# Graph attention kernel, first layer: a step's context is scaled on VectorE and added to the strip's sum on GpSimd

## The reference

```python
h = jnp.maximum(_layernorm(x, axis=-1), 0.0)
q, k, v = h @ Wq.T + bq, h @ Wk.T + bk, h @ Wv.T + bv      # split into 4 heads
kc = k.reshape(B, H, Nc, CHUNK, Dh)                          # 8 chunks of 256 keys
scores = jnp.clip(einsum('bhnd,bhjcd->bhnjc', q, kc) / sqrt(Dh), -10.0, 10.0)
scores = jnp.where(mask == 0, -10.0, scores)
attn = jax.nn.softmax(scores, axis=-1)                       # over each chunk by itself
ctx = jnp.einsum('bhnjc,bhjcd->bhnd', attn, vc)              # summed over the chunks
out = ctx @ Wo.T + bo + h                                    # then a layer norm, gamma, beta
x = x + out
```

## Time and profile before

| | |
|---|---|
| median of 3 runs | 4495.8 us (4494.7 to 4496.92) |
| the profiled execution's own time | 4492.85 us |
| its span, first to last instruction | 4491.0 us |
| PE busy | 4246.6 us (95%) |
| DVE busy | 4024.7 us (90%) |
| ACT busy | 2977.8 us (66%) |
| POOL busy | 714.7 us (16%) |
| granted TensorE clock, mean | 0.992 |

### The profile page before, as it was taken

The page is one execution under the profiler, slowest core; times in us unless marked ns, Lnnn a source line. Parts: engine busy times, 40 slices in busy tenths (PEclk is TensorE's granted clock), DMA queues, the critical chain, the costliest instruction groups (busy, mean ns, idle before and its releaser), DMA issues. The chain is left out here.

```text
span 4491.0 us, 168889 instructions
## 1 busy us (share of the span) xinstructions
PE 4246.6 (95%) x72733; PEld 3492.7 (78%) x72733; DVE 4024.7 (90%) x9728; ACT 2977.8 (66%) x3317; POOL 714.7 (16%) x613
## 2 busy tenths in 40 slices
PE   7999999999999999999999999969999999999998
PEld 5777777677677777777767777758999999999998
DVE  5998899889898899889988989978999999999998
ACT  5555555555555555555555555538999999999997
POOL 3121122112121122112211211110000010000100
PEclk9999999999999999999999999989999999999999
DMA  5100110011001010011011101113212122122221
GB/s 122 58 23 19 34 30 21 26 30 30 26 21 30 21 35 23 24 31 30 21 27 29 30 21 27 36 35 102 76 39 83 41 70 81 31 80 54 58 71 36
DMA packets 174046, 188.95 MB, mean 42 GB/s; under 512 B 7520, under 2 KB 157408, under 8 KB 173152
## 3 DMA queue, kind: packets, MB, share of 16 engines
q1 hardware_dynamic: 166192, 159.49, 12.8%
q0 software_dynamic: 7088, 18.36, 1.7%
HBM read 110.43 MB, written 38.03 MB: 33 GB/s over the span
## 5 line engine op out<-in xcount | busy, mean ns | idle before, releaser
L789 ACT ACTIVATE slot<-slot,shift 128x1024 f32<-128x1024 f32 x1024 | 1113.5, 1088 | 1184.5 <-PE slot L639 1176.2
L651 PEld LDWEIGHTS outs<-v_s,probs 128*64 128x64 f32 x32768 | 1042.2, 137 | 450.5 <-issue 271.3
L925 DVE SCALAR_TENSOR_TENSOR probs<-slot,bound 128x1024 f32<-128x1024 f32 x1024 | 1245.6, 1217 | 90.1 <-ACT slot L789 84.7
L651 PE MATMUL outs<-v_s,probs 128*64 128x66 f32 x32768 | 1179.5, 225 | 62.7 <-DVE ctx_sum L945 58.1
L1559 ACT ACTIVATE u<-s_all,d_sign 128x1024 bf16<-128x1024 f32 x1024 | 1117.7, 1139 | 57.0 <-PE sums L1460 39.1
L638 PE MATMUL slot<-q_hl,k_hl 128*128 128x512 f32 x2048 | 919.7, 449 | 59.1 <-DMA q_hl<-q_hl 35.9
L639 PE MATMUL slot<-q_hl,k_hl 128*128 128x512 f32 x2048 | 812.6, 397 | 0.0
L945 DVE SCALAR_TENSOR_TENSOR ctx_sum<-outs,inv,ctx_sum 128x64 f32<-128x64 f32 x3584 | 769.6, 278 | 31.7
L1456 PE MATMUL sums<-x_mixed,u 128*128 128x130 f16 x8192 | 785.7, 219 | 1.7 <-issue 1.5
L1460 PE MATMUL sums<-x_mixed,mask 128*128 128x65 f16 x8192 | 759.2, 193 | 4.6 <-issue 4.5
L1691 DVE TENSOR_TENSOR u<-u,mask 128x1024 f16<-128x1024 bf16 x1024 | 687.1, 681 | 76.8 <-ACT u L1559 68.2
(11 more groups left out here) (156 smaller groups left out, 3667.3 us busy)
## 6 DMA issues: line engine op xcount, KB each, us to landing
q_hl<-q_hl SPq DMA_DIRECT2D x128, 256.0 KB, 3.6
s_all<-s_turned SPq DMA_DIRECT2D x64, 512.0 KB, 5.6
x_q_s<-in_x SPq DMA_DIRECT2D x32, 512.0 KB, 5.1
x<-y SPq DMA_DIRECT2D x32, 512.0 KB, 3.2
t_o_s<-x SPq DMA_DIRECT2D x16, 1024.0 KB, 5.7
out<-t_o_s SPq DMA_DIRECT2D x16, 1024.0 KB, 6.7
x_q_s<-x SPq DMA_DIRECT2D x28, 512.0 KB, 6.1
probs<-in_adj POOLq DMA_DIRECT2D x12, 512.0 KB, 7.0
```

The lines of the kernel that those rows point to most:

```text
L651: end = nc.tensor.matmul(outs[i % OUTS][rows_of, q, 0:V_COLS], probs[:, i % PROBS, r, q * P + g * D:q * P + (g + 1) * D], v_s[:, c * JC + ...
L789: nc.scalar.activation(slot[:, :, :], slot[:, :, :], ACT.Exp, bias=shift[:, 0:1], scale=SCALE).then_inc(act_done, 1)
L925: nc.vector.scalar_tensor_tensor(probs[:, i % PROBS, :, :], spot(kind, "step", s, i)[:, :, :], P_LOW, bound[:, (i // H) % 2, :, :], ALU.ma ...
```

## The change

`scale` of the 28 later steps becomes one `tensor_tensor` of the form that the first four steps have; it writes one of four buffers `parts` instead of `ctx_sum`, and waits that the add of four steps earlier has read the buffer. GpSimd gets a new operation in each of these steps, `add_part`, which adds the buffer to `ctx_sum`. It counts a new semaphore `ctx_added`, and TensorE's `turn` waits on that. `values` still waits on `ctx_scaled`, which VectorE counts.

```diff
+PARTS = 4
+STRIP_ADDS = STEPS - H
...
+        parts = sb("parts", [P, PARTS, IT, D])
...
+            def add_part(b, s, i):
+
+                g = b * NS + s
+                pool.wait_ge(ctx_scaled, OUTS + g * STEPS + i + 1)
+                if i >= 2 * H:
+                    pool.wait_ge(ctx_added, g * STRIP_ADDS + i - 2 * H + 1)
+                nc.gpsimd.tensor_tensor(ctx_sum[:, :, i % H, :], ctx_sum[:, :, i % H, :], parts[:, i % PARTS, :, :],
+                                        ALU.add).then_inc(ctx_added, 1)
+
             def batch(b, kind):
...
                     for i in range(H, STEPS):
+                        add_part(b, s, i)
                         if has_before and i - H + 3 < Y_CHAIN:
                             finish(*before, i - H + 3, i - H + 4)
...
-                pe.wait_ge(ctx_scaled, OUTS + (g + 1) * STEPS)
+                pe.wait_ge(ctx_added, (g + 1) * STRIP_ADDS)
...
-                    dve.wait_ge(ctx_scaled, OUTS + g * STEPS + i - H + 1)
-                    for q in range(IT):
-                        op = nc.vector.scalar_tensor_tensor(ctx_sum[:, q, h, :], outs[i % OUTS][:, q, 0:D],
-                                                            inv[:, i % 2, q:q + 1], ctx_sum[:, q, h, :], ALU.mult, ALU.add)
-                    op.then_inc(ctx_scaled, 1)
+                    if s > 0 or kind != FIRST or i >= H + PARTS:
+                        dve.wait_ge(ctx_added, g * STRIP_ADDS + i - H - PARTS + 1)
+                    nc.vector.tensor_tensor(parts[:, i % PARTS, :, :], outs[i % OUTS][:, :, 0:D],
+                                            inv[:, i % 2, :].unsqueeze(2).to_broadcast([P, IT, D]),
+                                            ALU.mult).then_inc(ctx_scaled, 1)
```

More of the change, by code:

```diff
@@ L265, in layer0_block @@
         ctx_scaled = sem("ctx_scaled")
+        ctx_added = sem("ctx_added")
         y_stats_done = sem("y_stats_done")
```

## The result

The changed kernel takes 4432.72 us (median of 4 runs, 4432.22 to 4438.91) against 4496.36 us before (median of 4); the ratio is 0.9862 with a 95% interval of 0.9845 to 0.9879. So 63.6 us were won; 4433 us was forecast. The profiled execution took 4432.22 us, its span is 4430.4; between the two profiled executions the difference is 60.6 us.

What follows compares the result with a forecast made beforehand. TensorE was taken to set the pace, 2.21 us a step against VectorE's 2.11, waiting when side work made VectorE late. Gains of 52 + 4 + 7.5 = 63 us made 4430, plus 3 for the median: 4433 us, range 4417 to 4460.

Steps and rivals of the forecast that it cites:

- What bounds the kernel: Layer 0 steps: TensorE sets the pace at 2.21 us, VectorE at 2.11, leaving 0.10 a step for VectorE's side work.
- Waits that go: TensorE's waits for scale behind side work from iteration 18 on: all taken as gone, VectorE's step falling to about 1.67 us.
- The statistics' wait: TensorE's wait for scale behind the output statistics: shrinks by 0.44 us, about 0.35 stays in every strip.
- The add: GpSimd's 896 new adds of 128x256: 0.73 us each, bounds 0.42 and 1.28, 0.81 with the gap.
- Turn: At a strip's end TensorE's turn starts 0.37 us later, all lost, in 24 strips and at the layer's end.
- the control strip: Last batch's second strip, with no side work but output statistics: 81.15 us before, 81.08 forecast for a strip like it.
- The chain and the buffers: GpSimd's chain for y ends 3.2 us later; VectorE does not wait, tightest scale(12): chain 16.8 us, wanted at 17.7.
- The first batch's second strip: Its load, already waited for 3.16 us by VectorE, comes 3.2 us later; strip taken as no better than before.
- The last strip: Last batch's fourth strip: wins 2.6 us, from 4.4 of waits less 0.35 statistics, 1.0 chain and 0.4 turn.
- The term for the chain: In the last strip the inverse standard deviation stands behind six adds on GpSimd: 1 us taken as lost.
- The sum: Layer 0 gain: 52 us in six middle batches, 4 in the first, 7.5 in the last; 63 us in all.
- The range: Low end 4417 us, if the statistics' wait goes and adds reach their lower bound; high end 4460.

Runs made afterwards that it cites:

- the scaling issued twice: The changed kernel with the scaling operation issued twice in each of the 28 steps, once into an unused tile: 4496.13 us, ratio to before 1.0005.
- VectorE's own adds: The changed kernel with VectorE doing each add itself, one step later, as one 128x256 operation, and no add on GpSimd: 4550.64 us, ratio to before 1.0128.
- two buffers: The changed kernel with PARTS = 2 in place of 4: 4489.16 us, ratio to before 0.9991.
- doubled adds: The changed kernel with GpSimd's add issued twice in each step, once into an unused tile: 4507.43 us, ratio to before 1.0033.

## Why the prediction was right, point by point

- *What bounds the kernel.* TensorE's step of 2.21 us, VectorE's of 2.11, and the difference as what swallows side work: the scaling issued twice shows it, since one operation of 0.42 us more on VectorE alone undoes everything. The step fell to 1.77 in the loop and not to 1.67, which left enough.
- *Waits that go.* All waits behind iteration 18 were taken as gone. In the middle batches they are: in the third strip every step there without TensorE work of its own between is now 2.21 us. This is the gain, 54 us by the table above.
- *The statistics' wait.* Forecast to fall by 0.44 to about 0.35 in every strip. In the unrolled batches the step went from 3.07 to 2.64, so by 0.43; in the loop from 2.98 to 2.64, by 0.34, in three strips of four. What stays is 2.64 - 2.21 = 0.43. In the last strip of each of the six loop batches the step is 3.00; before, it took 2.98, so nothing was won. VectorE stands idle for half a microsecond between a reciprocal and the scaling there, at the same instruction in each pass:

```profile
1070.97 0.15 DVE L945 RECIPROCAL inv<-outs 128x4 f32<-128x4 f32 x1
...
1071.61 0.42 DVE L959 TENSOR_TENSOR parts<-outs,inv 128x256 f32<-128x256 f32 x1 [0.48 <-DVE inv L945]
```

  No engine is named but VectorE itself. The same pause stands a second time in each pass, at step 23 of the second strip, where TensorE loses nothing. With VectorE's own adds both pauses lie in the first strip, at steps 14 and 26, and with the scaling issued twice there is none. So they move with VectorE's instruction list; why they arise stays open. The one shown costs about 0.35 us in each of six batches and was not in the sum.
- *The add.* 733 ns in the median, 0.73 forecast from the line through two rows; that is 1.73 times VectorE's 424.
- *Turn.* It starts 0.45 us later against the start of the last scaling, for 0.37 forecast: the signal from VectorE to GpSimd takes 0.16 us (969.68 to 969.84) where I had used 0.08. But the forecast that all of it is lost was wrong. From the last `values` of a strip to the next strip's first TensorE takes 4.90 us for 4.59 in the middle strips of the loop, 0.31 more, and at the end of the control strip 4.65 for 4.65, nothing more. Before, the scores behind turn did not start when turn was through. They waited for a slot that `clip` had to free, and `clip` stood behind the long scaling. Before, in the earlier trace rows's strip end:

```profile
989.39 2.56 DVE L925 SCALAR_TENSOR_TENSOR probs<-slot,bound 128x1024 f32<-128x1024 f32 x2
...
990.66 0.19 PEld L638 LDWEIGHTS slot<-q_hl,k_hl 128*128 128x128 f32 x1 [0.20 <-DVE probs L925]
```

  and after:

```profile
971.52 0.19 PEld L652 LDWEIGHTS slot<-q_hl,k_hl 128*128 128x128 f32 x1
```

  From turn's start to these scores it was 1.05 us and is 0.82. The shorter scaling took that wait away too; this pays back part of turn's delay in the loop and all of it at the end of the control strip. The term of 0.37 in 24 strips, 9 us, was about 5.6 us in truth (18 times 0.31); the 1.8 us of the table's row hold chance waits as well.
- *The chain and the buffers.* VectorE never waits for `ctx_added`. `scale(12)` was named as the tightest, 0.9 us behind the add that it needs; in the trace of the change that margin is 0.91 us in the median and 0.80 at least, the smallest of all steps. With two buffers or doubled adds VectorE does wait, and the times came within 4 and 7 us of the same arithmetic. The ring of four is just enough: with three, by the times in this trace, the scaling of step 11 would come 1.3 us ahead of the add that it needs, an estimate that was not run.
- *The first batch's second strip.* The delay of the load came nearly as worked out: VectorE waited 5.88 us where the earlier trace rows had 3.16, 2.7 more for 3.2 forecast. Three steps took 7.56, 3.96 and 2.74 us for 5.27, 3.97 and 3.06, and the strip took 0.8 us more than before, where it was taken as even.
- *The last strip.* Forecast to win 2.6 us; it took 104.6 us from copy to copy and 105.9 before, so 1.3. The term for the chain, 1.0, was too small: two steps there took 6.52 and 6.34 us for 5.57 and 5.56, 1.7 more. The inverse standard deviation comes later, and two normalisations are locked out as well, one by each of two adds in a row. They take 1.53 us together, where they took 0.70 before. The waits, too, fell by less than forecast: several steps of this strip are still 2.33.

```profile
2867.67 1.45 POOL L494 TENSOR_TENSOR ctx_sum<-ctx_sum,parts 128x256 f32<-128x256 f32 x2
...
2867.74 1.53 DVE L860 TENSOR_SCALAR ahead<-t_o_s,moments,rstd 128x256 f32<-128x256 f32 x2
```

- *The sum.* From copy to copy layer 0 won 62.9 us, 63 forecast. The six loop batches won 51.7 (52), the first batch 4.8 (4), the last 6.4 (7.5). Inside them terms were off both ways: the first three strips of a loop batch won 7.7 us on average for 7.1, its last strip 0.9 for 1.5. So the mechanism was right, and that the total fits this well is partly luck. Luck is also that the median came out at the forecast: the forecast added 3 us to the profiled execution, as in the kernel before, and for the change this difference is 0.5; in its place layer 1, which was not touched, took 2.3 us more in the profiled execution (1491.0 to 1493.3 from the last copy to the end; the traces of this study have 1489.8 to 1495.2).
- *The range.* Its low end, 4417, is 2 us off its own terms: 29 x 0.35 + 25 x 0.31 = 18 us under 4433 make 4415. Nothing hangs on it.

## What to carry to other kernels

When one engine sets the pace by a small margin, the margin of the engine behind it per step is the number to work out. In this kernel, work taken from it was worth nothing in quiet steps, and nearly the whole gain came behind bursts of side work. Handing work to a slower engine that is mostly idle was free where its result is wanted late. Where a consumer waits for the last piece, the handoff stands in its way (here 1.0 us from the scaling's end to turn where it was 0.13, and 0.45 net of the shorter scaling); split that wait by what is really read first, and look at what else the consumer waits for behind it. Count the buffers against the receiving engine's worst stretch, not its mean load.

## What the runs showed of the hardware

An add on VectorE with two SBUF inputs waits for a GpSimd `tensor_tensor` that runs already: 415 ns in the median, up to 2224 beside the chain. The scaling, with an input in PSUM and one in SBUF, does not: 423 to 426 ns in 896 instances. A normalisation (`tensor_scalar`, SBUF to SBUF) waits for a GpSimd `tensor_tensor`, the residual's add, in 7 of 7 cases in the trace of the kernel before, 1218 to 1220 ns each. Beside GpSimd's `tensor_scalar` it mostly does not, which I had not expected: 21 of 25 took 401 to 411 ns. The other four, all in the first 236 us, took 685 to 698, and why is open. One of the 21:

```profile
1050.66 1.49 POOL L457 TENSOR_SCALAR h_q_s<-h_q_s 128x512 f32<-128x512 f32 x1
...
1051.12 0.41 DVE L846 TENSOR_SCALAR h_q_s<-x_q_s,moments,rstd 128x256 f32<-128x256 f32 x1
```

Between a reciprocal and the scaling that waits for it VectorE takes 0.21 us in the unrolled batches of the change and 0.29 in nearly all later steps of the loop's body; with the four operations of before it took 0.21 in both. Twelve distances, two in each pass of the loop, are 0.63 to 0.67. Why was not tried.
